# Block maxima of the wide activations: three more bf16 folds in place of a strided maximum

## The reference, cut to what matters

```python
def mx_quant(x):
    s = x.shape
    xb = x.reshape(s[:-1] + (s[-1] // BLOCK, BLOCK))
    amax = jnp.max(jnp.abs(xb), axis=-1, keepdims=True)
    shared_exp = jnp.floor(jnp.log2(jnp.where(amax > 0, amax, 1.0)))
    scale = jnp.exp2(shared_exp - (BITS - 2))
    q = jnp.clip(jnp.round(xb / scale), -2.0 ** (BITS - 1), 2.0 ** (BITS - 1) - 1) * scale
    ...
h = mx_linear(h, W1, b1)      # 256 -> 1024
h = mx_gelu(h)                # rounded to bf16
h = mx_linear(h, W2, b2)      # 1024 -> 256, quantises the 1024-wide h
```

## Time and profile before

| | |
|---|---|
| median of 3 timed runs | 292.58 us (292.56 to 328.08) |
| the profiled execution's own time | 291.33 us |
| its span, first to last instruction | 289.6 us |
| around the span | 1.7 us |
| TensorE busy | 270.8 us, 94% |
| VectorE busy | 261.2 us, 90% |
| ScalarE busy | 220.2 us, 76% |
| GpSimd busy | 174.1 us, 60% |
| mean granted TensorE clock | 0.988 |

### The profile page before, as it was taken

How to read it: one execution, slowest core, us unless ns; L and a number is a source line. 1 busy time by engine, 2 the same in 40 slices (tenths; PEclk the granted TensorE clock), 3 DMA queues, 4 the chain that set the end, 5 groups by cost and what they waited for, 6 DMA issues and landing times.

```text
span 289.6 us, 5338 instructions
## 1 busy us (share of the span) xinstructions
PE 270.8 (94%) x1640; PEld 165.4 (57%) x1640; DVE 261.2 (90%) x682; ACT 220.2 (76%) x378; POOL 174.1 (60%) x253
## 2 busy tenths in 40 slices
PE   8999998999997998999989998999699989997799
PEld 3776755477554764676566756575346444543454
DVE  3799999996999999999999999999986997799982
ACT  5131866479999699979998889889998899875650
POOL 2746380698466787868786878667777353533321
PEclk9999999999999999999999999999869999999999
DMA  7931200002110020022002200210010000100111
GB/s 239 381 125 36 65 3 0 9 6 71 37 43 0 8 71 15 1 67 77 16 1 63 79 9 5 66 44 9 7 36 5 3 0 0 37 3 1 37 38 38
DMA packets 11053, 12.68 MB, mean 44 GB/s; under 512 B 3216, under 2 KB 8336, under 8 KB 10768
## 3 DMA queue, kind: packets, MB, share of 16 engines
q1 hardware_dynamic: 10592, 11.55, 12.5%
q10 hardware_dynamic: 432, 0.79, 0.7%
HBM read 9.84 MB, written 2.10 MB: 41 GB/s over the span
## 4 chain that ended last, share of the span: by engine, by line
PE 44%; DVE 37%; issue 8%; ACT 6%; POOL 3%; DMA 1%; DVEq 0%; POOLq 0%
DVE nm L1323 9%; PE bank L2122 6%; PE bank L2156 6%; PE bank L2169 5%; DVE st L1278 4%; PE bank L2007 3%; PE bank L2235 3%; PE bank L2210 3%; PE bank L2056 2%; PE bank L2082 2%; DVE gq L1424 2%; PE bank L2069 2%; PE bank L2208 2%; ACT g_sb L877 1%; PE bank L2177 1%
## 5 line engine op out<-in xcount | busy, mean ns | idle before, releaser
L1323 DVE TENSOR_REDUCE nm<-bank 128x4 f32<-128x512 f32 x128 | 83.8, 677 | 0.8 <-PE bank L2122 0.6
L857 ACT ACTIVATE p_sb<-bank 128x512 f32<-128x512 f32 x128 | 72.3, 599 | 12.1 <-PE bank L2156 11.6
L2122 PE MATMUL bank<-kbd,xT 96*128 96x512 f32 x128 | 56.0, 468 | 2.6 <-ACT xT L828 1.5
L2156 PE MATMUL bank<-xT,kbd 104*128 104x512 f32 x128 | 53.0, 444 | 5.3 <-DMA xT<-mT 3.2
L555 POOL TENSOR_TENSOR kbd<-k3r,diag_sb 96x512 fp32r<-96x512 f32 x32 | 33.2, 1052 | 12.9 <-PE bank L2156 12.9
L2156 PEld LDWEIGHTS bank<-xT,kbd 104*128 104x128 f32 x128 | 24.6, 193 | 18.6 <-ACT p_sb L857 6.4
L2122 PEld LDWEIGHTS bank<-kbd,xT 96*128 96x128 f32 x128 | 24.4, 193 | 17.9 <-DVE nm L1323 10.8
L2169 PE MATMUL bank<-p_sb,va_sb 128*32 128x512 f32 x256 | 33.3, 610 | 0.0
L509 POOL TENSOR_TENSOR rs<-ve,nhalf 128x2 f32<-128x2 f32 (+1 forms) x36 | 26.1, 725 | 4.6
L504 POOL TENSOR_SCALAR ve<-mv 128x2 f32<-128x2 f32 (+1 forms) x36 | 8.4, 234 | 33.5 <-DVE mv L1284 31.8
L2043 PE MATMUL bank<-wkv_r,xt_r 128*128 128x512 f32 x84 | 23.8, 405 | 0.7 <-DVE r_sb L1301 0.7
(11 more groups left out here) (133 smaller groups left out, 619.1 us busy)
## 6 DMA issues: line engine op xcount, KB each, us to landing
xt_sb<-in_xt SPq DMA_DIRECT2D x8, 256.0 KB, 2.9
x_sb<-in_x SPq DMA_DIRECT2D x8, 256.0 KB, 2.9
out_dram<-o_sb SPq DMA_DIRECT2D x7, 256.0 KB, 2.2
k_sb<-in_ctx SPq DMA_DIRECT2D x8, 192.0 KB, 3.0
x_all<-in_w SPq DMA_DIRECT2D x1, 1024.0 KB, 6.2
w_raw<-in_w SPq DMA_DIRECT2D x1, 1024.0 KB, 8.3
p_sb<-in_wkv ACTq DMA_DIRECT2D x2, 256.0 KB, 3.9
cv_sb<-in_ctxv SPq DMA_DIRECT2D x8, 64.0 KB, 2.0
```

The costliest lines, as they stand in the source:

```text
L857: sc.activation(p_sb[:, k, :], bankB[k % 2][:, :], ACT.Exp, scale=SCORE_SCALE).then_inc(s_ex, 1)
L1323: ve.tensor_reduce(nm[:, b, u, g, :], bankA[(2 + k + 11 * b) % 2][:, :].rearrange("p (k t) -> p k t", k=KU), AX.X, ALU.max, negate=True).t ...
L2122: mm(bankA[(2 + k + 11 * b) % 2][:, :], xT[0:MR, b, u, g, :], kbd[0:MR, b, u, :, :].rearrange("r k t -> r (k t)"), start=True, stop=True). ...
L2156: mm(bankB[k % 2][:, :], kbd[0:MR + 2 * KU, b, u, kk, :], xT[0:MR + 2 * KU, b, u, :, :].rearrange("r g s -> r (g s)"), start=True, stop=Tr ...
```

## The change

The maximum over 8 strided values (i = 3) is replaced by three more folds, 256 to 128, 128 to 64 and 64 to 32 columns, all in bf16 (a maximum is exact there). The last one writes `am2`, which becomes bf16 in place of f32; the exponent bits are then cleared on 16-bit words. A sequence has 12 calls in place of 10. The three folds stand in a row wherever the reduce stood, with one call of another sequence moved by a place here and there in `head()` and `tail()`; the later calls are renumbered. The waits that counted calls (`gelu` waits until the batch's `g_sb` has been read) count the same work as before.

```diff
-FOLDS = 3
-GSTEPS = QSTEPS + FOLDS
+FOLDS = 6
+GSTEPS = FOLDS + 6
...
-        am2 = sb("am2", [P, PB, NBF], F32)
+        am2 = sb("am2", [P, PB, NBF], BF16)
...
-                    act.wait_ge(s_q2[b], GSTEPS * (p - 1) + FOLDS + 5)
+                    act.wait_ge(s_q2[b], GSTEPS * (p - 1) + FOLDS + 4)
...
+            def fold_g(b, i):
+                if i == 0:
+                    return ve.tensor_scalar(gz2[:, b, :].bitcast(U16), g_sb[:, b, :].bitcast(U16),
+                                            MAGNITUDE, None, ALU.bitwise_and)
+                into = am2 if i == FOLDS - 1 else gz2
+                n = F >> i
+                return ve.tensor_tensor(into[:, b, 0:n], gz2[:, b, 0:n], gz2[:, b, n:2 * n], ALU.max)
+
+            def scale_step(b, i):
+                am, sc, inv = am2[:, b, :], sc2[:, b, :], in2[:, b, :]
+                if i == 0:
+                    return ve.tensor_scalar(am.bitcast(U16), am.bitcast(U16), EXPONENT16, None, ALU.bitwise_and)
...
-                else:
-                    rows = F >> (FOLDS - 1)
-                    last = ve.tensor_reduce(am2[:, b, :], mag[:, 0:rows].rearrange("p (i k) -> p k i", k=NBF), AX.X, ALU.max)
...
                 quantise_g(0, 0, 3)
+                quantise_g(0, 0, 4)
+                quantise_g(0, 0, 5)
                 denominators(1, 1)
```

More of the change, by code:

```diff
@@ L33 @@
 EXPONENT = 0x7F800000
+EXPONENT16 = 0x7F80
 TINY = 2.0 ** -110
@@ L1449, in quantise_h, with scaled_step @@
                          hq[:, :], s_q1, i)
+            def fold_g(b, i):
[9 more added lines that the diff above has]
+                    return ve.tensor_scalar(am.bitcast(U16), am.bitcast(U16), EXPONENT16, None, ALU.bitwise_and)
+                if i == 1:
+                    return ve.tensor_scalar(sc, am, TINY, STEP, ALU.max, ALU.mult)
+                return ve.tensor_scalar(inv.bitcast(I16), sc.bitcast(I16), -1.0, INV_BITS, ALU.mult, ALU.add)
+            def scaled_step(b, i):
+                blocks = lambda t: t[:, b, :].rearrange("p (n i k) -> p n i k", n=1, i=BLK)
+                wide = lambda t: t[:, b, :].rearrange("p (n k) -> p n k", n=1).unsqueeze(2).to_broadcast([P, 1, BLK, NBF])
+                if i == 0:
+                    return ve.tensor_tensor(blocks(gz1), blocks(g_sb), wide(in2), ALU.mult)
+                if i == 1:
+                    return ve.tensor_scalar(blocks(gz2), blocks(gz1), QMAX, None, ALU.min)
+                return ve.tensor_tensor(blocks(gq), blocks(gz2), wide(sc2), ALU.mult)
             def quantise_g(p, b, i):
@@ L1453, in quantise_g @@
                     dve.wait_ge(s_g[b], p + 1)
+                else:
+                    dve.wait_ge(s_q2[b], GSTEPS * p + i)
                 if i == GSTEPS - 1 and later(p):
                     dve.wait_ge(s_gTp, 2 * (p - 1) + b + 1)
[L1456 to L1467, removed]
-                else:
-                    rows = F >> (FOLDS - 1)
-                    last = ve.tensor_reduce(am2[:, b, :], mag[:, 0:rows].rearrange("p (i k) -> p k i", k=NBF), AX.X, ALU.max)
+                if i < FOLDS:
+                    last = fold_g(b, i)
+                elif i < FOLDS + 3:
+                    last = scale_step(b, i - FOLDS)
+                else:
+                    last = scaled_step(b, i - FOLDS - 3)
                 last.then_inc(s_q2[b], 1)
@@ L1652, in head @@
                 quantise_g(0, 1, 3)
-                quantise_g(0, 0, 7)
                 quantise_g(0, 1, 4)
+                quantise_g(0, 1, 5)
+                quantise_g(0, 0, 9)
+                quantise_g(0, 1, 6)
                 mean_var(1, 1, st2, mv2, s_st2, s_mv2)
[L1656 to L1659, removed]
                 quantise_g(0, 1, 7)
+                quantise_g(0, 0, 10)
+                quantise_g(0, 1, 8)
+                quantise_g(0, 0, 11)
+                quantise_g(0, 1, 9)
                 k_times_v(4, 0)
@@ L1745, in step @@
                     quantise_g(p[4], 0, 3)
+                    quantise_g(p[4], 0, 4)
+                    quantise_g(p[4], 0, 5)
                 if on[3]:
@@ L1779, in step @@
                     quantise_g(p[4], 1, 3)
+                    quantise_g(p[4], 1, 4)
+                    quantise_g(p[4], 1, 5)
                 if on[3]:
@@ L1856, in tail @@
                 quantise_g(5, 1, 3)
+                quantise_g(5, 1, 4)
+                quantise_g(5, 1, 5)
                 maxima(7, 1, 4)
@@ L1859, in tail @@
                 maxima(7, 1, 5)
-                quantise_g(5, 1, 4)
-                quantise_g(5, 0, 8)
+                quantise_g(5, 1, 6)
+                quantise_g(5, 0, 10)
                 maxima(7, 1, 6)
@@ L1970, in tail @@
                 quantise_g(7, 1, 9)
+                quantise_g(7, 1, 10)
+                quantise_g(7, 1, 11)
                 last_x2(1)
```

78 lines of the change are left out of this document (43 added, 35 removed).

## The result

The changed kernel takes 295.84 us (median of 20 runs, 294.68 to 298.04), the kernel before 292.48 us (median of 20). The ratio is 1.0128, with a 95% interval of 1.011 to 1.0146 (an execution of the kernel before that took 328.08 us is left out of it): about 1.3% slower, within the 2% that was called "the same", and 0.1 us from the forecast of 295.7.

A forecast was written before the change was run, and what follows sets the result against it. VectorE and TensorE alternate on the chain of waits, so time added at the reduce adds to the kernel: 14 x 0.09 + 0.74 + 1.12 = 3.1 us on the median 292.58 gives 295.7 us, range 292.3 to 297.8.

The forecast's parts named there:

- small edits: Everywhere: `am2` in bf16 and the renumbered waits were said to cost nothing.
- hand-overs, 14 sequences: On VectorE, places without a wide GpSimd operation: three dependent folds occupy 0.575 us against the reduce's 0.49, +0.09 us each.
- head collision: In the head, the first fold stands behind GpSimd's `xt_r`: 0.93 us late, 0.74 after idle time at `nm`.
- tail collision: In the tail, folds stand behind GpSimd's `residual2`, released by the same `att`: `nm` starts 1.12 us later.
- The price of the folds: On VectorE: folds of 128, 64 and 32 columns estimated at 225, 193 and 177 ns, together 595 ns.
- The rival by which small folds are a gain: On VectorE: small folds are cheap, a wash or small gain, 291.0 to 293.0 us; chance 13%.
- The collisions: Head and tail: folds with two SBUF inputs stand still beside wide GpSimd operations, 0.74 and 1.12 us.
- The rival that they are hidden: Head and tail: collisions are hidden or don't happen, leaving 294.0 us, or 293.1 if half is absorbed; chance 30%.
- The delay of 0.93: In the head: the reciprocal behind the folds starts at 83.93 in place of 83.00, 0.93 us late.
- The clock rival: Behind the tail stall, 232 to 245 us: TensorE's clock falls, price 6.5 us in all, 299.1 us; chance 6%.

The follow-up runs named there:

- experiments two and three: Changed kernel with the reduce back in all sequences but one: folds only in the head (two), 292.97 us; only in the tail (three), 292.92 us.
- experiments nine and ten: Zero products in TensorE's gaps at 203 to 209 us: nine, changed kernel with head gap also filled, 296.91 us; ten, all reduces back, 293.36 us.
- experiments four and five: Changed kernel with reduce put back: four, in one head and one tail sequence, 293.32 us; five, everywhere but eight regular-step sequences, 291.92 us.

## Why the prediction was right

**The sum.** At like clocks, against the kernel before, in us:

| term | predicted | measured |
|---|---|---|
| small edits | 0 | -0.3 (291.06 - 291.35) |
| hand-overs, 14 sequences | 1.26 | 1.2 (293.08 - 291.89) |
| head collision | 0.74 | 1.0 (292.07 - 291.06) |
| tail collision | 1.12 | 1.1 (292.20 - 291.06) |
| sum | 3.1 | 3.0 |
| the whole change | 3.1 | 3.3 to 3.4 (294.68 - 291.35, and 294.74 - 291.35 with the head's gap filled) |
| clock fall at 90 to 95 us | not in the sum | 0.75 (295.49 - 294.74) to 1.1 (starts of the sequences) on top; all but one of 25 executions are below 0.988 |

*The price of the folds* held in the mean: 211, 192 and 174 ns for 225, 193 and 177, and 0.56 us for the place in the row where the reduce had 0.49. The straight line through two longer forms reached down to 32 columns. That all 14 places would pay 0.09 us did not hold: in the regular steps the first batches pay next to nothing and the second ones 0.14 to 0.20, half of it through `residual2` and the sign clearing, which the prediction didn't look at. That the mean comes out at 0.09 is in part luck. The rival by which small folds are a gain, with the advice to restructure a tensor_reduce, did not come: 579 ns of reduce became 211 + 192 + 174 = 577 ns of folds, and the hand-overs decide. The Trainium skill, "VectorE: DVE Perf Modes", section "Rules for kernel authors", also says for chained operations that their number should be kept small. Here that rule of the two was the one that the rows bore out.

*The collisions* came in the two places predicted and nowhere else among the folds. The tail's was 1.0 to 1.1 for 1.12. The rival that they are hidden fell with experiments two and three. (Its lower figure was also worked out wrongly: half of 1.4 us above 292.58 is 293.3, not 293.1.)

*What was mis-sized is the head.* The delay of 0.93 was right, but 0.58 of it rather than 0.74 was left behind `nm`, and then two things followed that were not looked at: the late `residual2` beside the next sign clearing (0.94 us for 0.43), and the longer gap of TensorE with its clock fall. Together, the head costs 1.0 us at like clock and up to 1.1 more where the clock falls.

*The clock rival* named the right mechanism in the wrong place. It was to act behind the tail stall; the clock there, 232 to 245 us, stayed at 1.00. It acted behind the head stall, where TensorE already had a gap of 1.45 us that the stall stretched. And its price of 3.4 us, read from the missing clock at 205 to 216 us, was far too high: experiments nine and ten gained nothing by giving it back, a dip there that was longer by 1.7 us of full speed (19 x 0.09) cost 0.57, and the fall in the head cost about a third of the 3.4.

*The total* is nearer than its parts deserve, by luck. The sum was added to a median of 292.58, in which one low-clock step was already contained in part; the changed kernel is one step or more down nearly always. The unpredicted clock fall (+1.1 against the profile) and the profile's luck (291.33 was an execution of the better clock) came out at the same place.

*Left open:* the 0.2 us by which the third regular step is longer than the others in the profiled execution; whether the 0.3 us by which the small edits seem to gain are more than chance (the ratio's interval has 1 in it); and which condition makes the clock fall in one execution of a kernel and not in the next, and in nearly all of the changed kernel where the head stall alone left at least a third of them without it.

## What to carry to other kernels

When a reduce is exchanged for elementwise operations with two SBUF inputs, first list GpSimd's wide operations beside each place: one meeting on the critical path (1.0 to 1.1 us) cost as much as twelve exchanges elsewhere (0.09 us each). Price a chain of small operations by its hand-overs and not by its columns alone; below 256 columns there was nothing left to gain from folds in a row. And when calls are moved to mend one meeting, look at what the movement brings beside GpSimd next: twice here, the stall went on to a neighbour.

## What the runs showed of the hardware that was not expected

- **The clock comes in steps.** Executions of one kernel have one of a few mean clocks (0.988, 0.982, 0.977, 0.971), about 1 us apart at the first step. With under 1% at stake, comparing executions at like clocks was sharper than comparing medians, once it was looked up where each lacks the clock: the changed kernel at 0.983 lacks it at 90 to 95 us, the kernels of experiments four and five at 0.982 lack more of it at 205 to 224.
- **A fall of the clock has no price of its own.** 3 us at 0.50 behind a gap of 2.4 us cost 0.75 to 1.1 us in the head; 1.7 us more of missing full speed between 205 and 224 us cost 0.57; filling the usual fall there gained nothing. VectorE is busy for 10.88 us of 205 to 216, TensorE for 8.71.
- **Small instructions stand still too.** A tensor_scalar on 32 columns took 0.78 us beside GpSimd, for 0.16 alone, and one on 1024 columns 0.94 for 0.43.
